# Gated cross-attention with an FFN on one core: scores of both batches in one pair, value products one tile late, variance two and FFN three tiles late inside the attention tiles, root as exp of half a log

## Chip, cores and metric

One Trainium2 chip, one core. The time is device microseconds of one execution; the kernel before has three runs and one further execution that was profiled. TensorE is called PE here, VectorE DVE, ScalarE ACT, GpSimd POOL, and SyncE SP; SP only issues DMAs.

## What is computed

`x` and `context` are 16 batches of 64 x 512 (fp32). In short:

```python
q, k = Wq @ inorm(lnorm(x)) + bq,  Wk @ inorm(ctx) + bk      # 64 x 512 per batch
v    = Ws @ ctx + bs
attn = softmax(q.T @ k)                                      # 512 x 512 per batch
mean, mean_sq = attn @ v, attn @ (v * v)
std  = sqrt(relu(mean_sq - mean * mean))
x    = x + tanh(g_xattn) * (inorm(ctx) * std + mean)
x    = x + tanh(g_ffn) * (lnorm(x) @ dequantised(weight_q).T)
```

## The kernel before

Two batches lie on the 128 partitions, so there are 8 **tiles** (t = 0 to 7). A tile's attention matrix is worked off in 8 **chunks** (c = 0 to 7) of 128 rows by 512 columns, chunks 0 to 3 of the first batch and 4 to 7 of the second. Every engine has its own program, a loop over tiles and chunks written out by hand, and semaphores tie them together; each engine takes its instructions strictly in the written order. Where a matrix is multiplied in fp32r, each operand is split into a high part `hi` and a rest `lo`, and three products (hi hi, hi lo, lo hi) replace one.

For a tile, `project` (PE) makes q and k, three products each. `keep_hi` (ACT) copies the high part out of PSUM, `keep_lo` (DVE) makes the rest. `scores` (PE) makes two chunks with six products; the two chunks run in the upper and the lower half of the array at the same time, and since both belong to the same batch, the other half needs a copy of q and k on the other partitions: `*_swapped`, made by DMAs of 128 KB that SP issues. `maximum` (DVE) takes the row maximum of a chunk, `exponentials` (ACT) the exp with its row sum, `reciprocal` (DVE) and `normalise_probs` (POOL) divide, `turn` (PE) transposes the chunk in four pieces, and `keep_turned` (ACT) copies the result from PSUM. `weigh` (PE, fp32) multiplies the turned probabilities with values and squared values. `value_product` (PE), `keep_values` (DVE) and `square_values` (POOL) make those. `keep_sums` (ACT) copies mean and mean square of one batch, each 64 x 512, into `MEAN` and `VAR`.

Then `with_mean`, `square_mean`, `variance` and `relu` run on DVE inside the next tile. The root (`root`, ACT), `scale_context` (POOL), `after_attention` and `row_statistics` (DVE), `inverse_deviation2` (POOL), `normalise_y` (ACT), `turn_y` (PE), `keep_y_hi` (ACT), `keep_y_lo` (DVE), the 12 products of `feed_forward` (PE) and `add_ffn` (DVE) all come behind the last attention tile, for all 8 tiles one after the other, because Sqrt is in another function table of ACT than Exp. The FFN weights are dequantised in tiles 6 and 7.

## Time and profile before

| | us |
|---|---|
| median of 3 runs | 201.22 (200.82 to 201.68) |
| the profiled execution, its own time | 201.95 |
| its span, first to last instruction | 200.1 |
| mean granted clock of PE | 0.991 |

The time of an execution is its span and what lies around it: 1.85 us here. The chain of waits names, for each moment of the span, what the end of the program was waiting for; the timeline gives the start and the length of each instruction of one engine, with the idle time before it and who ended that. Matmuls overlap their successors, so what one costs is read from start to start.

### The profile page before, as it was taken

The page shows a single profiled execution, that of the slowest core. Times are in us where ns is not written, and L with a number is a line of the kernel's source. Part 1 is how long each engine was busy: PE and PEld are TensorE (multiplying, and loading weights), DVE is VectorE, ACT ScalarE, POOL GpSimd, SP SyncE. Part 2 cuts the span into 40 slices and gives each one's busy share as a digit, 9 for nine tenths or more (in the row PEclk, how much of TensorE's full clock was granted, in tenths as well). Part 3 has the DMA queues.
Part 4 walks back from the last instruction along what each step waited for, and adds up shares of the span by engine and source line. Part 5 has one row for each costly group of instructions (what it writes and reads, how often), then busy time and mean ns, then how long its engine had stood idle before and what let it go on. Part 6 is the DMA issues. An engine that isn't in the chain of part 4 may idle for free.

```text
span 200.1 us, 2899 instructions
## 1 busy us (share of the span) xinstructions
PE 171.7 (86%) x816; PEld 106.3 (53%) x816; DVE 157.0 (78%) x337; ACT 127.1 (64%) x271; POOL 120.9 (60%) x143
## 2 busy tenths in 40 slices
PE   0359799999799979997997999799979893999993
PEld 0235556564465545554644565465446442787882
DVE  3868798779778976997699769955978687999751
ACT  2336767947776685959486948676594994563510
POOL 2125578458645754784487458685798957598300
PEclk9999999999999999999999999999999999699999
DMA  6247680773078127804760540073000000011322
GB/s 164 92 102 213 139 233 0 176 217 135 18 166 271 73 66 154 305 5 115 186 227 0 139 126 0 6 179 80 0 2 0 3 0 0 3 52 52 126 87 105
DMA packets 10880, 20.09 MB, mean 100 GB/s; under 512 B 1648, under 2 KB 1776, under 8 KB 10864
## 3 DMA queue, kind: packets, MB, share of 16 engines
q1 hardware_dynamic: 10864, 19.90, 35.3%
q8 instruction: 7, 0.11, 0.2%
q14 instruction: 9, 0.07, 0.1%
HBM read 9.67 MB, written 2.10 MB: 59 GB/s over the span
## 4 chain that ended last, share of the span: by engine, by line
PE 45%; DVE 26%; ACT 12%; issue 7%; DMA 3%; POOL 2%; SPq 2%; ACTq 0%; DVEq 0%
PE pv_bank L361 11%; PE score_bank L337 8%; ACT probs L484 6%; DVE neg_max L669 5%; PE turn_bank L348 5%; PE score_bank L438 4%; PE score_bank L439 4%; DVE VAR L693 4%; PE score_bank L442 4%; PE proj_bank L373 3%; DVE CTX L650 3%; DVE VAR L698 2%; ACT VAR L501 2%; DMA params_sb<-in_params 2%; DVE q_lo L663 2%
## 5 line engine op out<-in xcount | busy, mean ns | idle before, releaser
L886 POOL TENSOR_SCALAR probs<-probs,rden 128x512 f32<-128x512 f32 x64 | 56.4, 882 | 35.0 <-DVE rden L675 34.6
L484 ACT ACTIVATE probs<-score_bank,neg_max 128x512 f32<-128x512 f32 x64 | 44.3, 692 | 33.6 <-DVE neg_max L669 30.8
L361 PE MATMUL pv_bank<-probs_t,values 128*128 128x512 f32 x120 | 60.3, 604 | 0.9 <-ACT VAR L501 0.6
L669 DVE TENSOR_REDUCE neg_max<-score_bank 128x1 f32<-128x512 f32 x64 | 43.5, 681 | 20.3 <-PE score_bank L337 20.2
L348 PEld LDWEIGHTS turn_bank<-ident,probs 128*128 128x128 f32 x256 | 29.7, 142 | 26.7 <-issue 18.0
L348 PE MATMUL turn_bank<-ident,probs 128*128 128x128 f32 x256 | 37.6, 279 | 3.2 <-ACT probs_t L492 2.8
L492 ACT COPY probs_t<-turn_bank 128x512 f32<-128x512 f32 x64 | 37.3, 586 | 0.2
L361 PEld LDWEIGHTS pv_bank<-probs_t,values 128*128 128x128 f32 x120 | 19.7, 190 | 13.0 <-issue 12.5
L337 PE MATMUL score_bank<-k_hi,q_hi 64*128 64x512 f32 x32 | 16.6, 518 | 2.6 <-DVE k_lo_swapped L759 2.5
L337 PE MATMUL score_bank<-k_hi_swapped,q_hi_swapped 64*128 64x512 f32 x32 | 16.6, 518 | 0.0
L438 PE MATMUL score_bank<-w_hi,yt_hi 128*128 128x512 f32 x32 | 14.1, 440 | 0.0
L439 PE MATMUL score_bank<-w_lo,yt_hi 128*128 128x512 f32 x32 | 13.5, 423 | 0.0
L337 PE MATMUL score_bank<-k_lo_swapped,q_hi_swapped 64*128 64x512 f32 x32 | 13.0, 407 | 0.0
L337 PE MATMUL score_bank<-k_hi,q_lo 64*128 64x512 f32 x32 | 13.0, 407 | 0.0
L337 PE MATMUL score_bank<-k_lo,q_hi 64*128 64x512 f32 x32 | 13.0, 406 | 0.0
L337 PE MATMUL score_bank<-k_hi_swapped,q_lo_swapped 64*128 64x512 f32 x32 | 13.0, 406 | 0.0
L564 ACT ACTIVATE y<-X,shift,rstd 128x512 f32<-128x512 f32 x8 | 6.5, 817 | 9.9 <-POOL shift L969 9.9
L484 ACT ACTIVATION_READ_ACCUMULATOR probs<-score_bank,neg_max 128x1 f32 x64 | 12.8, 201 | 0.0
L675 DVE RECIPROCAL rden<-den 128x1 f32<-128x1 f32 x64 | 9.8, 153 | 3.5 <-ACT probs L484 2.9
L879 POOL TENSOR_TENSOR c_lo<-CTX,c_hi 128x512 fp32r<-128x512 f32 x7 | 8.9, 1271 | 5.2 <-DVE c_hi L656 5.2
L319 PE MATMUL proj_bank<-x_hi,w_qk_hi 128*128 128x512 f32 x8 | 4.6, 569 | 8.3 <-DVE x_lo L751 8.3
L337 PEld LDWEIGHTS score_bank<-k_hi,q_hi 64*128 64x128 f32 x32 | 6.2, 194 | 10.0 <-issue 6.3
(106 smaller groups left out, 343.1 us busy)
## 6 DMA issues: line engine op xcount, KB each, us to landing
X<-in_x SPq DMA_DIRECT2D x8, 256.0 KB, 3.1
CTX<-in_context SPq DMA_DIRECT2D x8, 256.0 KB, 3.4
q_hi_swapped<-q_hi SPq DMA_DIRECT2D x16, 128.0 KB, 2.3
q_lo_swapped<-q_lo SPq DMA_DIRECT2D x16, 128.0 KB, 2.4
ctx_now<-in_context SPq DMA_DIRECT2D x8, 256.0 KB, 2.6
sz<-in_scales_zeros SPq DMA_DIRECT2D x4, 512.0 KB, 4.9
out<-result SPq DMA_DIRECT2D x8, 256.0 KB, 2.0
k_hi_swapped<-k_hi SPq DMA_DIRECT2D x15, 128.0 KB, 2.4
```

Of the source, the lines that this page charges most:

```text
L337: mm = pe.matmul(score_bank[(c + half) % SBANKS][:, :], q_part[p][rows, P * j:P * j + P], k_part[p][rows, :], start=(step == 0), stop=(ste ...
L348: last = pe.transpose(turn_bank[c % 2][:, P * i:P * i + P], probs[c % SBANKS][:, P * i:P * i + P], ident[:, :])
L361: mm = pe.matmul(sums_bank(t, b)[:, :], values[:, i, b, :, :].rearrange("p a c -> p (a c)"), probs_t[b][:, i, :], start=(i == 0), stop=(i ...
L438: pe.matmul(score_bank[2 + i][:, :], hi, w_hi[:, g, :], start=(g == 0), stop=False)
L439: pe.matmul(score_bank[2 + i][:, :], hi, w_lo[:, g, :], start=False, stop=False)
L442: mm = pe.matmul(score_bank[2 + i][:, :], yt_lo[i][:, P * g:P * g + P], w_hi[:, g, :], start=False, stop=(g == GROUPS - 1))
L484: act.activation(probs[c % SBANKS][:, :], score_bank[c % SBANKS][:, :], ACT.Exp, bias=neg_max[:, c:c + 1], accum_out=den[:, c:c + 1]).then ...
L492: act.copy(probs_t[b][:, :, P * j:P * j + P], turn_bank[c % 2][:, :].rearrange("p (i n) -> p i n", i=JC)).then_inc(turned_kept, 1)
L669: dve.tensor_reduce(neg_max[:, c:c + 1], score_bank[c % SBANKS][:, :], AX_X, ALU.max, negate=True).then_inc(max_done, 1)
L675: dve.reciprocal(rden[:, c:c + 1], den[:, c:c + 1]).then_inc(rden_done, 1)
L879: pool.tensor_tensor(lo[:, :], whole, hi[:, :].bitcast(F32), ALU.subtract).then_inc(lo_done, 1)
L886: pool.tensor_scalar(probs[c % SBANKS][:, :], probs[c % SBANKS][:, :], rden[:, c:c + 1], 1.0, ALU.mult, ALU.mult).then_inc(probs_done, 1)
```

## The change

- `scores(t, p)` makes chunk pair p of **both** batches: batch 0 in the upper half of the array, batch 1 in the lower. The swapped copies, their buffers and their DMAs are gone. Chunk c now belongs to batch c % 2. A pair has a PSUM tensor of two banks (`score_banks`, two of them), and `maximum` takes both chunks in one instruction of 128 x 1024.
- `project` of q and k of tile t + 2 both stand at chunk 2 of tile t and write into `score_banks[0]`, which the scores of the pair before and after use too. So `scores(t + 1, 0)` at chunk 4 waits until `keep_lo` has read them.
- `weigh` of tile t - 1 is spread over the eight chunks of tile t. Behind the loop, `weigh` of tile 7 stands alone.
- Mean, variance and root of tile t - 2, and row statistics, stand inside tile t. Square of the mean moves from DVE to POOL; the casts `x_hi` and `c_hi` move from DVE to ACT (`split_hi`).
- The root is Exp(0.5 Ln(v)), with one function table loaded near the start by hand; v is floored at 2**-63.
- The FFN of tile t - 3 stands inside tile t: `normalise_y` at ACT's chunk 1, `turn_y` and `keep_y_hi` at chunk 2, `keep_y_lo` at chunk 3, `feed_forward` in halves at chunks 5 and 6, `add_ffn` at chunk 7. The FFN of tiles 5, 6 and 7 stands behind the loop.
- The weights are dequantised in tiles 1 and 2, the context is kept instead of loaded twice, and all loads are issued at the start.

```diff
-    AHEAD_S, AHEAD_E = 3, 2
-    SBANKS = 4
-    LAST = CHUNKS * TILES
+    AHEAD_E = 3
+    AHEAD_R = 2
+    PROBS = 6
     DMA = 16
...
+        score_banks = [banks(f"score_banks{i}", [P, 2, N]) for i in range(2)]
...
+            for t in range(1, 4):
+                load(t)
+            for g in range(GROUPS):
+                sp.dma_start(w_int[:, g, :], weight_q_t[P * g:P * g + P, :]).then_inc(ffn_w_loaded[g], DMA)
+                sp.dma_start(sz[:, g, :, :], scales_zeros[g].partition_broadcast(P)).then_inc(ffn_w_loaded[g], DMA)
+            for t in range(4, TILES):
+                load(t)
+            for u in range(TILES):
+                sp.wait_ge(result_done, u + 1)
...
+                elif t > 1:
+                    pe.wait_ge(exp_done, CHUNKS * (t - 2) + 6)
...
+            def scores(t, p):
+                number = PAIRS * t + p
+                if p == 0:
+                    pe.wait_ge(q_lo_done, t + 1)
                     pe.wait_ge(k_lo_done, t + 1)
-                if not (is_first(t) and c < SBANKS):
-                    pe.wait_ge(exp_done, CHUNKS * t + c + 2 - SBANKS)
-                for step, (q_whole, q_other, k_whole, k_other) in enumerate((
...
+                    if 2 <= t + 1 < TILES:
+                        pe.wait_ge(q_lo_done, t + 2)
+                        pe.wait_ge(k_lo_done, t + 2)
+                if number >= 2:
+                    pe.wait_ge(exp_done, 2 * (number - 2) + 2)
+                for step, (q, k) in enumerate(((q_hi, k_hi), (q_hi, k_lo), (q_lo, k_hi))):
+                    for b in range(2):
+                        rows = slice(C * b, C * b + C)
+                        mm = pe.matmul(score_banks[number % 2][:, b, :], q[t % 2][rows, P * p:P * p + P],
+                                       k[t % 2][rows, :], start=(step == 0), stop=(step == 2))
                         if step == 2:
                             mm.then_inc(scores_done, 1)
...
+                if c == 4 and t >= 3:
+                    pe.wait_ge(yt_hi_done, t - 2)
+                    pe.wait_ge(yt_lo_done, t - 2)
+                elif c == 6:
+                    pe.wait_ge(s_kept, t + 1)
+                elif CHUNKS * t + c >= 2:
+                    kept = {0: -1, 1: 0, 2: 1, 3: 3, 4: 2, 5: 5, 7: 6}[c]
+                    pe.wait_ge(turned_kept, CHUNKS * t + kept)
...
+                if (b, i) == (0, 0):
+                    pe.wait_ge(turned_kept, CHUNKS * (u + 1))
+                    pe.wait_ge(s_squared, u + 1)
...
+                    if u >= 1:
+                        pe.wait_ge(sq_kept, 2 * (u - 1) + 1)
+                    if u >= 3:
+                        pe.wait_ge(result_done, min(u - 2, TILES - 3))
...
+                pe.wait_ge(turned_kept, kept)
+                if u >= TILES - 1:
+                    pe.wait_ge(yt_hi_done, u - 1)
+                    pe.wait_ge(yt_lo_done, u - 1)
...
+                if 1 in steps:
+                    mm.then_inc(ffn_done, 1)
...
+            for t in range(TILES):
                 for c in range(CHUNKS):
-                    if c % 2 == 1 and c + AHEAD_S < CHUNKS:
-                        scores(t, c + AHEAD_S)
-                    elif c % 2 == 1 and has_next(t):
-                        scores(t + 1, c + AHEAD_S - CHUNKS)
-                    if c == 7 and has_second_next(t):
-                        pe.wait_ge(s_kept, 2 * t + 2)
+                    if c % 2 == 0:
+                        ahead = c // 2 + 2
+                        if ahead < PAIRS:
+                            scores(t, ahead)
+                        elif t + 1 < TILES:
+                            scores(t + 1, ahead - PAIRS)
+                    turn(t, c)
+                    if t > 0:
+                        weigh(t - 1, c // JC, c % JC)
+                    if c == 2 and t + 2 < TILES:
...
+                        project(t + 2, 1)
+                    if c == 2 and t >= 3:
+                        turn_y(t - 3, CHUNKS * t + 2)
+                    if c == 4:
                         value_product(t)
-            over_tiles(pe, body)
+                    if c == 5 and t >= 3:
+                        feed_forward(t - 3, 0)
+                    if c == 6 and t >= 3:
+                        feed_forward(t - 3, 1)
+            for i in range(JC):
+                weigh(TILES - 1, 0, i)
+            turn_y(TILES - 3, CHUNKS * TILES)
             for i in range(JC):
                 weigh(TILES - 1, 1, i)
...
+            feed_forward(TILES - 3, 0, 1)
+            turn_y(TILES - 2, CHUNKS * TILES)
+            feed_forward(TILES - 2, 0, 1)
+            turn_y(TILES - 1, CHUNKS * TILES)
+            feed_forward(TILES - 1, 0, 1)
...
+            def logarithm(u):
+                act.wait_ge(relu_done, u + 1)
+                act.activation(VAR[u % 2][:, :], VAR[u % 2][:, :], ACT.Ln).then_inc(log_done, 1)
...
-                act.activation(tile_of(VAR, u), tile_of(VAR, u), ACT.Sqrt).then_inc(root_done, 1)
+                act.wait_ge(log_done, u + 1)
+                act.activation(VAR[u % 2][:, :], VAR[u % 2][:, :], ACT.Exp, scale=0.5).then_inc(root_done, 1)
...
+            act.preload_act_table_set("natural_log_exp_and_others")
+            split_hi(0, 0)
+            split_hi(0, 1)
...
+            split_hi(1, 1)
+            exponentials(0, 0)
+            exponentials(0, 1)
+            keep_hi(1, 0)
+            keep_hi(1, 1)
+            exponentials(0, 2)
+            split_hi(2, 0)
+            split_hi(2, 1)
...
-                        keep_hi(t + 1, 1)
                     if c + AHEAD_E < CHUNKS:
                         exponentials(t, c + AHEAD_E)
...
+                    if c == 0 and t >= 2:
+                        keep_sums(t - 2, 1)
+                    if c == 4 and t >= 1:
                         keep_sums(t - 1, 0)
...
+                    keep_turned(t, c)
+                    if c == 1 and t >= 3:
+                        normalise_y(t - 3)
+                    if c == 2 and t >= 3:
+                        keep_y_hi(t - 3)
+                    if c == 3 and t + 2 < TILES:
                         keep_hi(t + 2, 0)
...
+                        keep_hi(t + 2, 1)
+                    if c == 5 and t >= 2:
+                        logarithm(t - 2)
+                        root(t - 2)
+                    if c == 6 and t + 3 < TILES:
+                        split_hi(t + 3, 0)
+                        split_hi(t + 3, 1)
...
+            keep_sums(TILES - 2, 1)
+            normalise_y(TILES - 3)
...
+            keep_y_hi(TILES - 3)
+            logarithm(TILES - 2)
+            root(TILES - 2)
             keep_sums(TILES - 1, 1)
-            root(5)
-            normalise_y(3)
-            root(6)
-            for u in range(2, TILES):
-                keep_y_hi(u, u % 2)
-                if u == 3:
-                    root(TILES - 1)
-                if u + 2 < TILES:
-                    normalise_y(u + 2)
+            normalise_y(TILES - 2)
+            logarithm(TILES - 1)
+            root(TILES - 1)
+            keep_y_hi(TILES - 2)
+            normalise_y(TILES - 1)
+            keep_y_hi(TILES - 1)
...
+            def maximum(t, p):
+                number = PAIRS * t + p
+                dve.wait_ge(scores_done, 2 * number + 2)
+                dve.tensor_reduce(neg_max[:, 2 * p:2 * p + 2], score_banks[number % 2][:, :, :], AX_X, ALU.max,
                                   negate=True).then_inc(max_done, 1)
...
+                    if c + AHEAD_R < CHUNKS:
+                        reciprocal(t, c + AHEAD_R)
+                    elif t + 1 < TILES:
+                        reciprocal(t + 1, c + AHEAD_R - CHUNKS)
+                    if c % 2 == 0:
+                        ahead = c // 2 + 2
+                        if ahead < PAIRS:
+                            maximum(t, ahead)
+                        elif t + 1 < TILES:
+                            maximum(t + 1, ahead - PAIRS)
+                    if c == 0 and t + 3 < TILES:
+                        statistics(t + 3, 0)
+                    if c == 1:
+                        if t + 3 < TILES:
+                            statistics(t + 3, 1)
+                        if t >= 2:
+                            with_mean(t - 2)
...
+                        if t >= 3:
+                            keep_y_lo(t - 3)
+                        if t >= 2:
+                            variance(t - 2)
+                        if t + 2 < TILES:
                             keep_lo(t + 2, 0)
...
+                            keep_lo(t + 2, 1)
+                    if c == 4 and t >= 2:
+                        relu(t - 2)
+                    if c == 5:
+                        keep_values(t)
+                        if t + 3 < TILES:
+                            normalise(t + 3, 0)
+                            normalise(t + 3, 1)
+                    if c == 7:
+                        if t >= 3:
+                            add_ffn(t - 3)
+                        if t >= 2:
+                            after_attention(t - 2)
+                            row_statistics(t - 2)
...
+            with_mean(TILES - 2)
+            variance(TILES - 2)
+            relu(TILES - 2)
+            keep_y_lo(TILES - 3)
+            after_attention(TILES - 2)
+            row_statistics(TILES - 2)
+            with_mean(TILES - 1)
+            variance(TILES - 1)
+            relu(TILES - 1)
```

On PE, the stretch around the projection of k, before. `proj_bank` holds the projection; the scores behind it are those of another pair, in another bank.

```order
L361 MATMUL pv_bank<-probs_t,values 128x512
L348 MATMUL turn_bank<-ident,probs 128x128 x8
L319 MATMUL proj_bank<-c_hi,w_qk_hi 128x512
L320 MATMUL proj_bank<-c_lo,w_qk_hi 128x512
L321 MATMUL proj_bank<-c_hi,w_qk_lo 128x512
L337 MATMUL score_bank<-k_hi_swapped,q_hi_swapped 128x512
L337 MATMUL score_bank<-k_hi,q_hi 128x512
L337 MATMUL score_bank<-k_lo_swapped,q_hi_swapped 128x512
L337 MATMUL score_bank<-k_lo,q_hi 128x512
```

The same stretch on PE in the changed kernel, in a tile with an FFN: the projection, `turn_y`, one transposed chunk, one `weigh` product and the next tile's first scores.

```order
L220 MATMUL score_banks<-c_hi,w_qk_hi 128x512
L221 MATMUL score_banks<-c_lo,w_qk_hi 128x512
L222 MATMUL score_banks<-c_hi,w_qk_lo 128x512
L293 MATMUL turn_bank<-ident,y 128x128 x4
L255 MATMUL turn_bank<-ident,probs 128x128 x4
L273 MATMUL sums_bank<-probs_t_0,values 128x512
L238 MATMUL score_banks<-k_hi,q_hi 128x512 x2
L238 MATMUL score_banks<-k_lo,q_hi 128x512 x2
L238 MATMUL score_banks<-k_hi,q_lo 128x512 x2
```

The projection's banks are now the banks of the scores four rows behind it. In between stand only eight transposes of 128 columns and one product of 512.

On ACT, before: `keep_hi` of q (L473), then exponentials, and `keep_hi` of k (L477) five rows on.

```order
L484 ACTIVATE probs,den<-score_bank,neg_max 128x512
L492 COPY probs_t<-turn_bank 128x4x128
L473 ACTIVATE q_hi<-proj_bank,params_sb 128x512
L484 ACTIVATE probs,den<-score_bank,neg_max 128x512
L500 COPY MEAN<-pv_bank 64x512
L501 COPY VAR<-pv_bank 64x512
L492 COPY probs_t<-turn_bank 128x4x128
L477 ACTIVATE k_hi<-proj_bank,params_sb 128x512
```

On ACT in the changed kernel, the same kind of stretch (chunks 2 and 3 of a tile with an FFN). L429 is `keep_y_hi`, L397 `keep_turned`, L372 `keep_hi`.

```order
L388 ACTIVATE probs,den<-score_banks,neg_max 128x512
L397 COPY probs_t_0<-turn_bank 128x4x128
L429 CAST yt_hi<-turn_bank 128x512
L388 ACTIVATE probs,den<-score_banks,neg_max 128x512
L397 COPY probs_t_1<-turn_bank 128x4x128
L372 ACTIVATE q_hi<-score_banks,params_sb 128x512
L372 ACTIVATE k_hi<-score_banks,params_sb 128x512
```

Both `keep_hi` now stand next to each other, behind a cast that waits for `turn_y`, an exponential, and a copy that waits for the transposed chunk 3.

On ACT behind the loop in the changed kernel, from the cast of the FFN of tile 5 to the end.

```order
L429 CAST yt_hi<-turn_bank 128x512
L412 ACTIVATE VAR<-VAR 128x512
L416 ACTIVATE VAR<-VAR 128x512
L407 COPY MEAN<-sums_bank 64x512
L408 COPY VAR<-sums_bank 64x512
L422 ACTIVATE y<-X,shift,rstd 128x512
L412 ACTIVATE VAR<-VAR 128x512
L416 ACTIVATE VAR<-VAR 128x512
L429 CAST yt_hi<-turn_bank 128x512
L422 ACTIVATE y<-X,shift,rstd 128x512
L429 CAST yt_hi<-turn_bank 128x512
```

L412 and L416 are log and root, first of tile 6, then of tile 7; `keep_y_hi` of tile 6 stands behind the root of tile 7.

## Rows read from the trace of the kernel before

**Rows 1.** The page, busy time of each engine over the span.
```profile
PE 171.7 (86%) x816; PEld 106.3 (53%) x816; DVE 157.0 (78%) x337; ACT 127.1 (64%) x271; POOL 120.9 (60%) x143
```

**Rows 2.** Windows: busy time of PE, PEld, DVE, ACT, POOL; clock; DMA.
```profile
71.92:90.76 18.84, 17.41 (x86) 10.21 (x86) 15.54 (x35) 13.48 (x31) 11.67 (x14) 1.00 0.50 140
165.30:200.10 34.80, 28.25 (x128) 22.37 (x128) 25.74 (x56) 13.59 (x21) 17.07 (x23) 0.95 0.16 61
```

**Rows 3.** Chain of waits in tile 5: start, length, engine, what.
```profile
109.25 0.67 DVE q_lo L663
...
110.01 0.47 PE proj_bank L319
...
110.95 0.89 PE score_bank L337 x6
...
112.43 1.72 PE pv_bank L361 x4
114.14 0.44 PE turn_bank L348 x4
...
115.44 0.89 PE proj_bank L373 x8
...
117.29 0.70 DVE neg_max L669
...
122.19 0.60 DVE mean_sq L687
...
123.47 1.59 DVE VAR L693
...
127.10 0.96 DVE VAR L698
```

**Rows 4.** Timeline of ACT in tile 3: start, length, instruction.
```profile
73.31 0.69 ACT L477 ACTIVATE k_hi<-proj_bank,params_sb 128x512 fp32r<-128x512 f32 x1 [0.28 <-PE proj_bank L321]
73.90 0.68 ACT L484 ACTIVATE probs<-score_bank,neg_max 128x512 f32<-128x512 f32 x1
...
74.56 0.58 ACT L492 COPY probs_t<-turn_bank 128x512 f32<-128x512 f32 x1
```

**Rows 5.** Timeline of PE at the start.
```profile
13.63 0.79 PE L337 MATMUL score_bank<-k_hi,q_hi 64*128 64x512 f32 x1 [2.47 <-DVE k_lo_swapped L759]
...
33.79 1.04 PE L348 MATMUL turn_bank<-ident,probs 128*128 128x128 f32 x8
```

**Rows 6.** Chain of waits behind tile 7.
```profile
158.66 1.28 ACT L506
...
159.95 0.63 ACT VAR L506
...
162.15 1.55 POOL CTX L960
...
163.73 1.75 DVE X L713
...
168.26 0.82 ACT y L564
...
180.87 0.44 PE score_bank L428 x4
...
184.10 0.44 PE score_bank L428 x4
...
196.84 0.75 DVE result L840
```

**Rows 7.** Timeline of PE behind tile 7, idle time in brackets.
```profile
167.71 0.63 PE L428 MATMUL score_bank<-ident,y 128*128 128x128 f32 x4 [2.41 <-ACT y L564]
...
169.83 0.64 PE L438 MATMUL score_bank<-w_hi,yt_hi 128*128 128x512 f32 x1
...
174.25 0.60 PE L428 MATMUL score_bank<-ident,y 128*128 128x128 f32 x4
```

**Rows 8.** The page, costliest groups: POOL's division of a chunk.
```profile
L886 POOL TENSOR_SCALAR probs<-probs,rden 128x512 f32<-128x512 f32 x64 | 56.4, 882 | 35.0 <-DVE rden L675 34.6 <-issue 0.3
```

879 lines of the change are left out of this document (318 added, 561 removed).

## The prediction, made before the changed kernel was run

> **What bounds the kernel now.** The busy times of the page come first [rows 1]: PE 86%, DVE 78%, the others about 60%. That is an average over unlike stages, so the windows come next [rows 2]. A middle tile lasts 18.84 us, DVE is busy for 15.5 of it, ACT 13.5, POOL 11.7. Behind tile 7 there are 34.8 us in which PE is busy 28.3. The chain of waits then prices PE's steps [rows 3]: a pair of scores 0.89, a turned chunk 0.44, four passes of `weigh` 1.72, which are two of its products (fp32 takes two passes), so 0.86 each, and a value product 0.89. A projection runs from 110.01 to 110.95, 0.94 where PE had idled before it, so 1.6 for two in a row. A tile has 4 x 0.89 + 8 x 0.44 + 8 x 0.86 + 0.89 + 1.6 = 16.4 us on PE. The other 2.4 us are waits, the largest for `q_lo` [rows 3], which DVE makes behind variance (1.59) and relu (0.96). So PE bounds the tiles, with one late link from ACT and DVE.
>
> **The same products, elsewhere.** The count of matmuls does not change. An FFN costs 184.10 - 180.87 = 3.23 us on PE [rows 6]. It leaves the end and makes tiles 3 to 7 longer: 16.4 + 3.2 = 19.6. The change gains only if waits become fewer. By capacity the others fit: to the windows of [rows 2] DVE adds the FFN's rest and sum, residual and statistics (about 3.5, at 0.6 to 0.75 each as in [rows 3, 6]) and loses two casts and a square (about 2), which makes 17; ACT adds two casts, log, root, y and its cast, some 3.8, which makes 17.3; POOL adds a square, a scaling (1.55, [rows 6]) and two powers, some 3.5, which makes 15. All stay under 19.6. What decides is the order.
>
> **The link at chunk 4.** `project` writes into the banks that `scores(t + 1, 0)` needs. Count from P, the end of both projections. In tiles 1 and 2 PE has a turn and a `weigh` to do, 0.44 + 0.86 = 1.3 us. Meanwhile ACT cannot start `keep_hi` before it has copied chunk 3, turned at P + 0.6, so the copy (0.58) ends at P + 1.15; `keep_hi` twice at a pitch of 73.90 - 73.31 = 0.59, the second ends at P + 2.4 [rows 4]; `keep_lo` of k 0.67 and a semaphore: P + 3.2. PE waits 1.9. In tiles 3 to 5 `turn_y` stands in front (P + 0.6), ACT casts it (0.5), then takes exponential 6 (0.66), the copy of chunk 3 (0.5), `keep_hi` twice (1.3), DVE takes `keep_lo` (0.7), and semaphores add 0.15: P + 4.4. PE has 1.74 us of work, so it waits 2.7. Exponential 6 could run earlier only if it stood ahead of the cast, which it does not. This wait takes the place of the one for `q_lo` and is as long.
>
> Elsewhere in a tile the chain just fits: residual and statistics of tile t - 3 end 1.3 us into the next tile, the two-chunk maximum (2 x 0.60, a little less than 0.70 twice) ends at 2.6, exponentials 4 and 5 with `normalise_y` between them at 5.4, and the projection wants them at 5.7. I add 0.3 per tile for this. The double maximum saves some 0.1 a pair on DVE, which is not waited for: nothing. The DMAs that go (swapped copies) held only tile 0 back.
>
> **Start.** Before, the first scores run at 13.63, after two swapping copies of 0.8 in series [rows 5]. These go, but the second table load stands before the cast of x: 1.28 us by row [rows 6]. The two cancel; first scores again at 13.6. The Trainium skill ("ScalarE: Activation LUTs", What ACT_TABLE_LOAD costs) puts a switch of tables at 2.66 us with its drain; here the next activation starts 0.01 us behind the 1.28. By the page the start would be 1.4 us later. Then tile 0, counted down each queue: maximum of the first pair 16.3, of the second, behind a set of statistics, 18.4, first division on POOL 20.3 (behind a second set), DVE's `keep_lo` and `normalise` of tiles 1 and 2 until 22.3, POOL's two rests of tile 2 (1.27 each, an estimate next to its 1.55) until 24.9, turned chunk 2 at 26.1, projections of tile 2 at 27.8, next scores at 30.9, and 4.5 us for the rest of tile 0: tile 1 starts at **35.4**. Before, that point is 33.79 + 0.44 = 34.2 [rows 5].
>
> **Sum.** Tile 1: 16.4 + 1.9 at chunk 4 + 1.4 because `weigh` of tile 0 waits for its last copied chunk = 19.7. Tile 2: 16.4 + 1.9 + 0.5 (POOL has weights, rests and square there, some 18 to 19 us) = 18.8. Tiles 3 to 5: 19.6 + 2.7 + 0.3 = 22.6 each, 67.8. Tile 6 without projection: 16.4 - 1.6 + 3.2 + 0.2 = 18.2. Tile 7, two pairs of scores fewer: 16.4. The loop ends at 35.4 + 19.7 + 18.8 + 67.8 + 18.2 + 16.4 = **176.3**.
>
> Behind it `weigh` of tile 7 and one `turn_y` take 7.3, and ACT copies the sums until 8.7. But tile 7 queues behind tile 6: cast for tile 5 at 5.3, log and root of tile 6 (2 x 0.63) 6.6, scaling, residual, statistics, power 10.7, then POOL squares tile 7's mean 11.8, variance and relu 13.0, log and root 14.3. From scaling to y the chain of before took 162.15 to 169.08, 6.9 us, with the residual at 1.75 and another tile's statistics in it [rows 6]; freed of these I count 4.9: y at 19.2. Turn 0.6, cast 0.6, twelve products 2.9, sum 0.75: 24.2. The store and end are 200.1 - 197.6 = 2.5. PE idles about 2.8 us ahead of the FFN of tile 6. Before, it idled 2.41, turned a tile, and ran at half rate from 169.83 to 174.25, 4.4 us for what takes 2.8 at full rate [rows 7]; the granted clock of the stretch is 0.95, that of a tile 1.00 [rows 2], so PE fell from 2.4 to 1.2 GHz for that time. I take 1.2 us, since the last FFN may be back at full rate. The tail is 27.9, the span 176.3 + 27.9 = **204.2**. The profiled execution of before was 201.95 with a span of 200.1, and the median 0.73 under it: 204.2 + 1.85 - 0.73 = **205.3 us**, 2% slower. The bounds: the tail's 4.9 may be 6.9 (+2) or the clock may stay up (-1.2); the waits of six tiles are together 15 us, and half a microsecond each way is 3; tile 0 is known to about 2. Added as squares that is about 4: 201 to 209.5 for this case alone.
>
> **Rivals.**
> *Faster.* The wait at chunk 4 is short. It holds if ACT and DVE run ahead enough that `keep_lo` of k ends by P + 2; then tiles are 19.7 with FFN, six waits of 1.9 to 2.7 become 0.3, which takes 12 us off: 193. For it speaks the spare capacity; against it, that copy and both `keep_hi` must follow P in any case, 3 us of rows. Half of it is possible, 199. It decides from 0.7 us less in each of six tiles on: that is the 4 us to the time of before. Chance 0.2.
> *No change.* Waits at chunk 4 of 2 instead of 2.7, tail without the half rate: 201 to 202. Chance 0.15.
> *DVE and POOL slow each other.* Two products of one shape take 0.60 and 1.59 in before, and POOL's division 0.88 in the mean [rows 3, 8]. With more on both, residual and with_mean at 1.75 would lie on the way to exponential 5: 1 us more in each of five tiles and in the tail: 211. That two-input DVE work and POOL share their way to SBUF is also what the Trainium skill says ("GPSIMD Engine Reference", Key points). Against it: most of what stands there reads PSUM. Chance 0.15.
> *The clock falls inside tiles.* The wait of 2.7 is longer than the 2.41 of [rows 7]. If PE falls to half rate behind it, a tile loses about 2: 210. Chance 0.1.
> *The root does not do what it says*, tables reloaded around each log: two loads of 1.28 a tile on ACT. The instructions in order hold only two loads in all. Below 0.01.
> The forecast keeps 0.4.
>
> **How the numbers follow.** A difference under 0.5% can't be told from none with this kernel. Faster by more: 0.2, from the first rival. Same: 0.15. Slower: 0.65. The range is 197 to 211: it leaves out the deeper half of the first rival and the worst of the slow ones.
>
> **What would show it.** In the trace after: PE waits of 1.9 (tiles 1, 2) and 2.7 us (3 to 5) in front of the first scores of a tile, ended by `keep_lo` of k; tile starts about 22.6 apart in tiles 3 to 5; tile 1 starting at 35; 28 us behind tile 7's last turned chunk, with ACT's root and POOL's scaling on the chain. Wrong if tiles are near 20 apart, or if the wait at chunk 4 is ended by something else.

## The result

The changed kernel takes **226.35 us** (median of 4 runs, 226.26 to 226.62); beside it the kernel before took 201.30 (200.82 to 201.68). The ratio is 1.125, 95% interval 1.122 to 1.127. The forecast was 205.3 us with a range of 197 to 211: the direction was right, the loss six times as large as forecast (25.0 us against 4.1). The profiled execution took 226.42 us, with a span of 224.4. Medians here and below are of all runs of a kernel; ratios and their intervals leave out single executions that were over 1.5% above the kernel's fastest.

The page of the kernel after, to be held against [rows 1]:

```profile
span 224.4 us, 2734 instructions
## 1 busy us (share of the span) xinstructions
PE 179.9 (80%) x816; PEld 112.2 (50%) x816; DVE 135.2 (60%) x275; ACT 138.5 (62%) x292; POOL 119.2 (53%) x149
...
PEclk9999576999998899979996799969999999999589
```

No engine is busy for a larger share than before; DVE's share fell from 78% to 60%. So this is not a kernel with too much work on one engine. The last line is the one to look at: the granted clock drops again and again between the start and the tail (a 5, 6, 7 or 8 among the 9s).

Tiles, as windows from the first `scores(t, 2)` of a tile to that of the next (tiles 2 to 6, last row: behind the loop). Columns as in [rows 2]: window, length, busy time of PE, PEld, DVE, ACT, POOL, granted clock, DMA share, GB/s.

```profile
59.45:80.56 21.11, 18.52 (x88) 10.69 (x88) 16.78 (x30) 15.31 (x35) 17.93 (x19) 0.92 0.00 1
80.56:107.72 27.16, 22.21 (x103) 13.37 (x102) 18.71 (x35) 17.68 (x40) 19.19 (x22) 0.94 0.00 1
107.72:133.56 25.84, 23.07 (x103) 14.65 (x102) 15.81 (x34) 16.77 (x37) 13.64 (x17) 0.87 0.03 11
133.56:158.09 24.53, 21.76 (x103) 13.70 (x102) 12.32 (x26) 15.84 (x35) 10.99 (x14) 0.93 0.03 11
158.09:176.77 18.68, 18.68 (x98) 11.43 (x97) 10.92 (x24) 14.68 (x33) 9.78 (x13) 1.00 0.04 14
...
193.80:224.40 30.60, 19.80 (x66) 12.09 (x64) 13.40 (x28) 10.45 (x17) 7.62 (x10) 0.89 0.09 35
```

Forecast were 18.8 us for tile 2, 22.6 for tiles 3 to 5, 18.2 for tile 6, 27.9 for the tail. Tile 6 fits. Tiles 2 to 5 are 2.3, 4.6, 3.2 and 1.9 us longer, and those are the tiles with a clock under 1.00. Tile 4 shows why. PE's timeline there (start, length, instruction, in brackets its idle time and who ended it):

```profile
115.01 0.60 PE L293 MATMUL turn_bank<-ident,y 128*128 128x128 f32 x4
115.44 0.60 PE L255 MATMUL turn_bank<-ident,probs 128*128 128x128 f32 x4
115.88 1.02 PE L273 MATMUL sums_bank<-probs_t,values 128*128 128x512 f32 x2
119.67 0.79 PE L238 MATMUL score_banks<-k_hi,q_hi 64*128 64x512 f32 x2 [2.77 <-DVE k_lo L518]
120.24 0.66 PE L238 MATMUL score_banks<-k_lo,q_hi 64*128 64x512 f32 x2
120.66 0.66 PE L238 MATMUL score_banks<-k_hi,q_lo 64*128 64x512 f32 x2
121.25 1.12 PE L255 MATMUL turn_bank<-ident,probs 128*128 128x128 f32 x4
122.16 1.92 PE L273 MATMUL sums_bank<-probs_t,values 128*128 128x512 f32 x2
123.87 1.92 PE L282 MATMUL turn_bank<-params_sb,CTX 128*128 128x128 f32 x8
```

Two things stand in these rows. The projections end at P = 115.01 and the next scores start at P + 4.66, behind a wait of 2.77 us that `k_lo` ends; forecast were P + 4.4 and 2.7. Behind the wait every product takes about twice as long: turning a chunk goes from 0.60 to 1.12, `weigh` from 1.02 to 1.92. PE had idled, and came back at 1.2 GHz instead of 2.4: from 119.7 to 125.6 us the granted clock is 0.50. The chain of waits gives the steps of the link:

```profile
116.91 0.48 ACT probs_t L397
117.39 0.60 ACT q_hi L372
...
118.01 0.75 DVE q_lo L518
118.76 0.67 DVE k_lo L518
...
119.67 1.62 PE score_banks L238 x5
```

It is the chain that the prediction counted. All six such waits: 2.91, 2.04, 2.59, 2.77, 2.77, 2.77 us (tiles 0 to 5), 15.85 in sum, all ended by `k_lo`. The low clock follows those of tiles 0, 2, 3, 4 and 5, and not that of tile 1, the shortest.

### The profile page after: what moved, and what is told of

Its sections match the earlier page's. It is cut to its first block, busy times and chain, and to the rows that moved or that the text cites. A ratio compares the mean times of both kernels' runs of the same rounds, so it can differ in the third digit from the quotient of the medians.

```text
span 224.4 us, 2734 instructions
## 1 busy us (share of the span) xinstructions
PE 179.9 (80%) x816; PEld 112.2 (50%) x816; DVE 135.2 (60%) x275; ACT 138.5 (62%) x292; POOL 119.2 (53%) x149
## 3 DMA queue, kind: packets, MB, share of 16 engines
q1 hardware_dynamic: 4752, 9.67, 11.8%
## 4 chain that ended last, share of the span: by engine, by line
PE 55%; DVE 17%; issue 9%; ACT 7%; POOL 7%; DMA 2%; SPq 0%; ACTq 0%; POOLq 0%; DVEq 0%
PE sums_bank L273 15%; PE turn_bank L255 11%; PE score_banks L238 11%; PE turn_bank L282 4%; DVE k_lo L518 2%; DVE neg_max L524 2%; DVE q_lo L518 2%; DMA params_sb<-in_params 2%; POOL CTXN L733 2%; ACT q_hi L372 2%; PE sums_bank L320 2%; PE sums_bank L314 2%; ACT probs L388 1%; PE score_banks L314 1%; DVE CTXN L511 1%
## 5 line engine op out<-in xcount | busy, mean ns | idle before, releaser
L273 PE MATMUL sums_bank<-probs_t,values 128*128 128x512 f32 x128 | 67.7, 620 | 1.0 <-ACT probs_t L397 1.0
L397 ACT COPY probs_t<-turn_bank 128x512 f32<-128x512 f32 x64 | 37.4, 585 | 39.5 <-PE turn_bank L255 39.3
L524 DVE TENSOR_REDUCE neg_max<-score_banks 128x2 f32<-128x1024 f32 x32 | 38.8, 1212 | 19.8 <-PE score_banks L238 19.8
L388 ACT ACTIVATE probs<-score_banks,neg_max 128x512 f32<-128x512 f32 x64 | 44.3, 693 | 7.5 <-DVE neg_max L524 7.2
L255 PEld LDWEIGHTS turn_bank<-ident,probs 128*128 128x128 f32 x256 | 31.6, 151 | 24.4 <-issue 12.6
L238 PE MATMUL score_banks<-k_hi,q_hi 64*128 64x512 f32 x64 | 17.4, 534 | 18.5 <-DVE k_lo L518 17.5
L238 PEld LDWEIGHTS score_banks<-k_hi,q_hi 64*128 64x128 f32 x64 | 6.7, 200 | 38.1 <-DVE q_lo L518 20.2
L273 PEld LDWEIGHTS sums_bank<-probs_t,values 128*128 128x128 f32 x128 | 20.8, 200 | 4.7 <-issue 2.9
L238 PE MATMUL score_banks<-k_hi,q_lo 64*128 64x512 f32 x64 | 14.4, 435 | 0.0
L733 POOL TENSOR_TENSOR CTXN<-CTXN,VAR 128x512 f32<-128x512 f32 x8 | 10.2, 1273 | 7.7 <-ACT VAR L416 7.7
L238 PE MATMUL score_banks<-k_lo,q_hi 64*128 64x512 f32 x64 | 14.2, 431 | 0.0
L282 PEld LDWEIGHTS turn_bank<-params_sb,CTX 128*128 128x128 f32 x64 | 10.9, 241 | 5.3 <-issue 5.3
L536 DVE TENSOR_TENSOR values<-turn_bank,params_sb 128x512 f32<-128x512 f32 x8 | 5.5, 691 | 13.2 <-PE turn_bank L282 13.2
L388 ACT ACTIVATION_READ_ACCUMULATOR probs<-score_banks,neg_max 128x1 f32 x64 | 13.1, 205 | 0.0
L282 PE MATMUL turn_bank<-params_sb,CTX 128*128 128x128 f32 x64 | 10.6, 320 | 0.0
```

The costliest lines, as they stand in the source:

```text
L238: mm = pe.matmul(score_banks[number % 2][:, b, :], q[t % 2][rows, P * p:P * p + P], k[t % 2][rows, :], start=(step == 0), stop=(step == 2))
L255: last = pe.transpose(bank[:, P * i:P * i + P], probs[(CHUNKS * t + c) % PROBS][:, P * i:P * i + P], ident[:, :])
L273: mm = pe.matmul(sums_bank[b][:, :], values[u % 2][:, i, b, :, :].rearrange("p a c -> p (a c)"), probs_t[u % 2][b][:, i, :], start=(i == 0 ...
L282: last = pe.matmul(turn_bank[0][:, P * i:P * i + P], CTX[:, t, P * i:P * i + P], w_s, start=True, stop=True)
L388: act.activation(probs[g % PROBS][:, :], score_banks[(g // 2) % 2][:, g % 2, :], ACT.Exp, bias=neg_max[:, c:c + 1], accum_out=den[:, c:c + ...
L397: act.copy(probs_t[t % 2][b][:, :, P * j:P * j + P], bank[:, :].rearrange("p (i n) -> p i n", i=JC)).then_inc(turned_kept, 1)
```

## The experiments

**Theory.** The wait in front of a tile's first scores costs twice: its own length, and the half rate behind it. **Rivals:** DVE and POOL slow each other, and the clock only mirrors the idle time; the FFN inside the tiles is simply too much work. Each kernel below is the changed kernel with small edits, from "The weights, elsewhere" on always on top of both halves of the link moved; "P" is again the end of both projections of a tile. The kernel before ran beside them (medians of 201.3 to 201.6).

### Fill the wait, keep the order

Added on PE (work for nothing; the results are those of the kernel):

```diff
+            def fill(t, n):
+                pe.wait_ge(k_lo_done, 2)
+                if t >= 2:
+                    pe.wait_ge(sq_kept, 2 * (t - 1))
+                for _ in range(n):
+                    pe.matmul(sums_bank[1][:, :], w_qk_hi[:, 0, :], q_hi[(t + 1) % 2][:, :], start=True, stop=True)
...
+                    if c == 3 and t + 2 < TILES:
+                        fill(t, (13, 8, 8, 12, 12, 12)[t])
```

> The kernel after, with 8 to 13 products of 512 columns added on PE at the end of chunk 3 of tiles 0 to 5, into a bank that is free then; nothing reads them, so they are work for nothing. They fill most of the wait in front of the next tile's first scores and leave the order of everything else. Main theory (the wait costs twice: its own 2.0 to 2.9 us, and the clock that falls behind it): the scores start as late as before, counted from the projections, but run at full rate; granted clock 1.00 in tiles 2 to 5 instead of 0.87 to 0.94; tile 4 falls from 25.8 to about 23, and the whole from 226.3 to about 214 (some 2.9 us in each of tiles 0, 3, 4 and 5, 1.6 in tile 2). Rival 1 (what is slow is DVE and POOL in each other's way; the clock only mirrors idle time): tiles stay as long, 226. Rival 2 (the added products hold something up, since sums_bank[1] or the queue was not free): above 226.

Measured: **216.19 us** (215.05 to 218.65), ratio 1.071 [1.065, 1.077]. PE in tile 4:

```profile
108.90 0.60 PE L300 MATMUL turn_bank<-ident,y 128*128 128x128 f32 x4
...
110.23 3.37 PE L291 MATMUL sums_bank<-q_hi,w_qk_hi 128*128 128x512 f32 x12
113.57 0.50 PE L238 MATMUL score_banks<-k_hi,q_hi 64*128 64x512 f32 x2
113.88 0.42 PE L238 MATMUL score_banks<-k_lo,q_hi 64*128 64x512 f32 x2
114.11 0.42 PE L238 MATMUL score_banks<-k_hi,q_lo 64*128 64x512 f32 x2
114.46 0.66 PE L255 MATMUL turn_bank<-ident,probs 128*128 128x128 f32 x4
```

The scores start at P + 4.67, where they started before, so the link is as late as it was. But they run 0.23 us apart instead of 0.42, and the tile takes 22.9 us instead of 25.8. From those scores to the `weigh` of chunk 5 it is 3.57 us against 6.51: the half rate cost 2.9 us in this tile. PE did more work, the link came no earlier, and 10 us went away over the kernel. The rival by which the clock only mirrors idle time is out. The Trainium skill ("TensorE: Matmul & The Clock Gate", Wait — 56ns, not 53.3ns?) gives 426.7 and 215.7 ns from start to start of products of 512 columns at the two clocks; the pitch of 0.42 us agrees, that of 0.23 is 7% above the page's.

The same reading for all six tiles, from a tile's first scores (those of tile t + 1) to the end of its window: 6.33, 8.17, 9.78, 12.50, 13.89 and 12.58 us in the kernel after, 4.80, 8.18, 8.16, 10.95, 10.95 and 10.96 with the fill. The half rate costs 1.5 to 1.6 us in tiles 0, 2, 3 and 5, 2.9 in tile 4 and nothing in tile 1: **9.3 us** together. The profiled execution with the fill also reached `scores(0, 2)` 0.85 us earlier (17.22 against 18.07), where nothing was changed; starts differ that much from one execution to the next.

### Fill it in doses

The same edit with `(0, 0, 0, 3, 6, 9)` products.

> The kernel after, with 3, 6 and 9 products added (work for nothing, as in e1_fill) at the end of chunk 3 of tiles 3, 4 and 5, none in tiles 0 to 2: the wait of 2.77 us in front of the next scores is cut to about 2.1, 1.5 and 0.8. Theory (half rate follows the wait, and only a long one): behind 0.8 and 1.5 the scores run at full rate, tiles 4 and 5 at 22.9 instead of 25.8 and 24.5; behind 2.1 it may go either way, since behind 2.04 it stayed and behind 2.09 it fell in earlier runs. Whole 226.35 - 1.6 - 2.9 = about 222, or 220 if tile 3 is freed too. Rival (any idle time at that place makes PE fall): tiles as in after, 226.

Measured: 222.93 us median; its four runs lie far apart (218.08 to 226.03), so the time alone decides little. The profiled one took 220.44. The first scores behind tiles 3, 4 and 5 in it:

```profile
94.83 0.50 PE L238 MATMUL score_banks<-k_hi,q_hi 64*128 64x512 f32 x2 [2.08 <-DVE k_lo L527]
...
117.73 0.51 PE L238 MATMUL score_banks<-k_hi,q_hi 64*128 64x512 f32 x2 [1.37 <-DVE k_lo L527]
...
140.64 0.50 PE L238 MATMUL score_banks<-k_hi,q_hi 64*128 64x512 f32 x2 [0.67 <-DVE k_lo L527]
```

Behind 2.08, 1.37 and 0.67 all is at full rate, and tiles 4 and 5 take 22.90 each. In this execution three products (0.7 us) in tile 3 were enough to keep the clock, while tile 2 of the same run, with its wait of 2.60, fell to half rate as ever. The rival that any idle time there makes PE fall is out. That these doses always suffice is not shown: two of the four executions took 225.43 and 226.03 us with a mean granted clock of 0.93, as the kernel after has, and of those there is no trace.

### Move ACT's half of the link

```diff
-                    if c == 2 and t >= 3:
-                        keep_y_hi(t - 3)
-                    if c == 3 and t + 2 < TILES:
+                    if c == 2 and t + 2 < TILES:
                         keep_hi(t + 2, 0)
                         keep_hi(t + 2, 1)
+                    if c == 2 and t >= 3:
+                        keep_y_hi(t - 3)
```

> The kernel after, with only ACT's two casts keep_hi moved from chunk 3 to chunk 2, ahead of keep_y_hi; DVE keeps its order (keep_y_lo, variance, keep_lo twice in chunk 3). Main theory: in tiles 0 to 2, with no y to cast, the casts end at P + 1.2 instead of P + 2.4, the scores wait 0.7 to 1 us instead of 2.0 to 2.9, and the clock does not fall: 1.3 less in each and 3 and 1.6 us of half rate less in tiles 0 and 2. In tiles 3 to 5 the cast of y now stands behind both, and DVE's rest of y and variance stand ahead of keep_lo, so the wait stays near 2.7 and half rate stays behind it. Whole about 218. Rival (ACT alone makes the link): all six waits shrink to under 1, whole about 205. Rival (the clock falls for another reason than this wait): half rate stays in tiles 0 and 2, about 222.

Measured: **218.8 us** (217.12 to 219.5), ratio 1.084 [1.078, 1.091]. The waits are now 1.33, 0.47, 2.09, 2.81, 2.37, 2.37. In tiles 0 and 1 the link is short, as expected. In tile 2 it is 2.09, more than the 0.7 to 1 I had written: there `variance` (1.10 us) already stands ahead of `keep_lo` on DVE. In tiles 3 to 5 DVE's order holds the link, as its chain behind tile 4 shows:

```profile
109.64 0.58 ACT yt_hi L429
...
110.86 0.68 DVE VAR L549
111.54 0.66 DVE q_lo L518
112.20 0.67 DVE k_lo L518
...
113.11 1.19 PE score_banks L238 x3
```

Both casts end early, and `keep_lo` still waits for the rest of y and for variance. The rival by which ACT alone makes the link is out. Half rate stays behind 2.81, 2.37, 2.37, and here behind 2.09 too (the turned chunk at 66.02 us takes 1.11).

### Move both halves

The edit above, and on DVE:

```diff
+                    if c == 2 and t + 2 < TILES:
+                        keep_lo(t + 2, 0)
+                        keep_lo(t + 2, 1)
                     if c == 3:
...
-                        if t + 2 < TILES:
-                            keep_lo(t + 2, 0)
-                            keep_lo(t + 2, 1)
```

> The kernel after, with keep_hi on ACT and keep_lo on DVE both moved to chunk 2, ahead of the cast and the rest of y and of variance. Same work, another order. Main theory: k_lo ends at P + 2.0, PE has 1.3 to 1.9 us of work until then, so the wait is under 0.5, PE stays at full rate, and both costs go: tiles 3, 4, 5 at about 21.5, 20.2, 20 us, tile 1 starts at 33 to 34, whole about 199 (15.8 us of waits and some 12 of half rate less). Rival 1 (the half rate is not a consequence of the wait): only the waits go, about 210. Rival 2 (capacity or contention of DVE and POOL is the bound behind the link): the waits come back elsewhere in the tile, 218 or more.

Measured: **204.97 us** (204.52 to 206.86), ratio 1.019 [1.012, 1.025]. PE behind tile 4's projections, to be held against the rows of the kernel after:

```profile
103.31 0.60 PE L293 MATMUL turn_bank<-ident,y 128*128 128x128 f32 x4
103.75 0.60 PE L255 MATMUL turn_bank<-ident,probs 128*128 128x128 f32 x4
104.18 1.02 PE L273 MATMUL sums_bank<-probs_t,values 128*128 128x512 f32 x2
105.24 0.50 PE L238 MATMUL score_banks<-k_hi,q_hi 64*128 64x512 f32 x2
```

No wait: the scores start at P + 1.93. On DVE the two rests go ahead of that of y:

```profile
103.55 0.75 DVE L518 SCALAR_TENSOR_TENSOR q_lo<-score_banks,params_sb,q_hi 128x512 fp32r<-128x512 f32 x1 [0.82 <-ACT q_hi L372]
104.23 0.75 DVE L518 SCALAR_TENSOR_TENSOR k_lo<-score_banks,params_sb,k_hi 128x512 fp32r<-128x512 f32 x1
...
104.97 0.67 DVE L586 TENSOR_TENSOR yt_lo<-turn_bank,yt_hi 128x512 fp32r<-128x512 f32 x1
```

Four instructions a tile in another place give back 21.4 of the 25 us, with the same work. Tiles 3 and 4 as windows:

```profile
71.65:96.03 24.38, 20.93 (x103) 12.46 (x103) 19.59 (x37) 18.52 (x41) 20.18 (x23) 1.00 0.00 1
96.03:116.19 20.16, 20.13 (x103) 12.61 (x103) 15.77 (x34) 16.89 (x37) 13.66 (x17) 1.00 0.04 14
```

Tile 4 is now PE's own work, 20.13 busy of 20.16, near the 19.9 that the prediction counts without the wait. It is 6 us more than the 199 expected: tile 3 takes 24.4 instead of 21.5, and tile 1 starts at 35.5 instead of 33 to 34. Tile 3 is the one place where capacity shows: POOL is busy for 20.2 of it and DVE for 19.6, and PE waits there for POOL:

```profile
79.31 0.66 PE L255 MATMUL turn_bank<-ident,probs 128*128 128x128 f32 x4 [1.12 <-POOL probs L706]
...
81.69 0.47 PE L220 MATMUL score_banks<-x_hi,w_qk_hi 128*128 128x512 f32 x1 [0.87 <-ACT probs L388]
```

The same two waits, 1.12 and 0.87, stand in the kernel after (at 86.70 and 89.09). Two more stand in front of them here, 0.59 and 0.83 for chunks 0 and 1; in the kernel after, chunk 1 waits for 0.19. In all PE waits 3.4 us in this tile.

### The weights, elsewhere

The weights in tiles 0 and 1 instead of 1 and 2 (DVE's part; POOL's `dequantise` and `weights_lo` likewise):

```diff
-                    if t in (1, 2):
+                    if t in (0, 1):
                         if c in (1, 5):
-                            scale_weights(2 * (t - 1) + c // 4)
+                            scale_weights(2 * t + c // 4)
```

> The order of the kernel before this one (casts and rests at chunk 2), and the weights of the FFN dequantised in tiles 0 and 1 instead of 1 and 2. Theory: the waits for POOL's probabilities at the start of tile 3 (1.12 and 0.19 us, 0.87 for an exponential) come from the last weights at the end of tile 2 and go, but part returns in tile 1: 1 to 2 us under the kernel with the link alone, about 197.5. Rival: those waits come from tile 3's own work, and nothing changes (within 0.5 us), or tile 0, where POOL is late already, gets longer by as much as tile 3 gains.

Measured: **202.76 us** (201.95 to 204.15), ratio 1.007 [1.003, 1.010]. Tile 3 falls from 24.38 to 20.36, tile 1 grows from 18.62 to 20.91: both sentences of the expectation hold in part, and 2.2 us stay. Not all of tile 1's growth is the weights' work. The kernel of "Behind the last tile" has the same tile 1, and the two traces show the `weigh` of its first chunk behind the same wait, the first line here, the second there:

```profile
38.17 2.04 PE L273 MATMUL sums_bank<-probs_t,values 128*128 128x512 f32 x2 [0.96 <-ACT probs_t L397]
37.27 1.12 PE L273 MATMUL sums_bank<-probs_t,values 128*128 128x512 f32 x2 [0.96 <-ACT probs_t L397]
```

Here PE ran on at half rate until about 42 us (granted clock 0.57 from 38 to 42), there it did not (1.00), and that tile 1 takes 19.68. So the weights cost tile 1 about 1.1 us, and half rate another 1.2, in some executions only. Then the four groups placed in the first halves of tiles 0 and 2 and both halves of tile 1:

```diff
+    GROUP_AT = [(0, 0), (1, 0), (1, 1), (2, 0)]
...
-                    if t in (0, 1):
+                    if (t, c // 4) in GROUP_AT:
                         if c in (1, 5):
-                            scale_weights(2 * t + c // 4)
+                            scale_weights(GROUP_AT.index((t, c // 4)))
```

> The kernel e4_link_weights with only the four groups of weights placed elsewhere: the first halves of tiles 0 and 2, both halves of tile 1 (there they were the halves of tiles 0 and 1). In the runs so far tile 3 took 24.4 us with a group in the second half of tile 2 and 20.4 without, tile 1 took 20.9 with one in the second half of tile 0 and 18.6 without; tile 2, behind a group in the second half of tile 1, took the same either way. Theory (a group that POOL and DVE work on across a tile's boundary holds up the next tile's probabilities, and tiles 0 and 2 have no room for it): tiles 1, 2, 3 at 18.6, 17.5, 20.4, whole 202.8 - 2.2 = about 200.5. Rival (each group costs the same wherever it is): 202.8.

Measured: 202.96 us (201.31 to 204.69), ratio 1.003 [1.000, 1.007]: nothing over the placement before. Tiles 1 and 2 take 18.63 and 17.51 as expected, but tile 3 is 21.89 and not 20.4, with a wait of 1.20 for an exponential. My rule, that only a group across a tile's boundary costs, is wrong in that form. The 2.3 us by which tile 1 is shorter hold the 1.2 of half rate, so the work itself gained 1.1 there and lost 1.5 in tile 3.

### Behind the last tile

POOL and DVE there, with the weights as in the first of the two placements:

```diff
-            with_mean(TILES - 1)
             variance(TILES - 1)
             relu(TILES - 1)
+            with_mean(TILES - 1)
...
-            inverse_deviation2(TILES - 2)
             square_mean(TILES - 1)
+            inverse_deviation2(TILES - 2)
```

> The kernel e4_link_weights with another order behind the last tile only: POOL squares tile 7's mean ahead of the power for tile 6 (it waited for that power from 178.9 to 181.7), and DVE takes variance and relu of tile 7 ahead of adding its mean. Theory (the tail is a chain through POOL's and DVE's queues, not PE's work): mean_sq ends at 180.0 instead of 182.8, the cast of y for tile 6 follows 1.5 us earlier, and y of tile 7 comes 2.5 to 3 us earlier; PE idles 2 instead of 3.5 us ahead of the FFN of tile 6. Whole 202.8 - 3 = about 199.8. Rival (PE bounds the tail: FFN at half rate): the last FFN starts no earlier than the one before it ends, gain under 1 us, 202.

Measured: **200.29 us** (199.1 to 202.7), ratio 0.990 [0.984, 0.995]. POOL in the kernel without this edit:

```profile
180.52 0.99 POOL L739 TENSOR_TENSOR rstd<-var_eps,power 128x1 f32<-128x1 f32 x1 [2.06 <-DVE var_eps L571]
...
181.72 1.04 POOL L728 TENSOR_TENSOR mean_sq<-MEAN 128x512 f32<-128x512 f32 x1
```

and with it:

```profile
176.78 1.21 POOL L728 TENSOR_TENSOR mean_sq<-MEAN 128x512 f32<-128x512 f32 x1 [0.48 <-ACT MEAN L407]
178.36 1.01 POOL L739 TENSOR_TENSOR rstd<-var_eps,power 128x1 f32<-128x1 f32 x1 [0.37 <-DVE var_eps L571]
```

Counted from the last turned chunk (168.83 and 166.68), `mean_sq` of tile 7 starts 10.1 instead of 12.9 us behind it, and the tail is 30.4 instead of 32.2 us. These 1.8 us are the edit's; the rest of the difference between the two traces lies ahead of it, 0.9 in the start and tile 0, 1.2 in tile 1's half rate. PE idles 1.95 instead of 3.50 us ahead of the FFN of tile 6, and that FFN is still at half rate for most of its length. Both edits together:

> Both edits of e5_tail and e6_spread. If they act in different places they add: 202.8 - 3.0 - 2.2 = about 197.6, under the 201.3 of the kernel before all changes; if the new order of work (FFN in the tiles, root by exp and log) costs more than it gives once its waits are gone, it stays at or over 201.

Measured: 201.40 us (200.66 to 202.95), ratio 0.999 [0.995, 1.002]. The tail's order takes 1.6 us off this placement too (202.96 to 201.40). But the expected 197.6 is missed: the new placement of the weights brings nothing here either.

### Dummy work at the start and in the tail

```diff
+            pe.wait_ge(ident_ready, 1)
+            for _ in range(40):
+                pe.matmul(turn_bank[1][:, 0:P], ident[:, :], ident[:, :], start=True, stop=True)
             pe.wait_ge(w_split, 1)
             project(0, 0)
```

> The kernel e7_both with 40 products of the identity with itself (128 columns, nothing reads them) on PE ahead of the first projection, while it has nothing else to do (from about 1.5 us to 8.4 us). In the runs so far PE starts at half rate at 8.4 us and stays there until 17.7. Theory (PE comes up to 2.4 GHz by having worked, whatever the work): projections and first scores run at full rate, the first scores start about 1 us earlier, tile 0 by 2; whole about 2 us under e7_both, 195.6. Rival (the low rate at the start belongs to the first microseconds, not to idleness): the start keeps its half rate and the products delay it, 0 to 2 us over e7_both.

Measured: 202.76 us (201.39 to 204.72), ratio 1.002 [0.999, 1.006]. The 40 products ran from 1.55 to 13.2 us and held the first projection up, which then took 0.40 instead of 0.63 us a product. So the rate was full behind them, as the theory had it, and the delay ate up what that gave. With 22 of them, ahead of the kernel with the new tail:

> The kernel e5_tail with 22 products of the identity with itself (nothing reads them) on PE ahead of the first projection. In e8_head_fill 40 of them ran from 1.55 to 13.2 us at full clock, about 0.29 us each, so they held the first projection up by 5 us, but what followed them ran at full rate and the whole was only 1.4 us longer. Now 22 should end at 8 us, when the first operand is ready. Theory: projections and first scores at full rate, first scores 1.2 us earlier, tile 0's second half free of the half rate; whole 1.5 to 2.5 us under e5_tail's 200.3, about 198.3. Rival (head waits for DVE and POOL, not for PE): within 0.5 us of e5_tail.

Measured: 199.77 us (198.55 to 201.62), ratio 0.992 [0.989, 0.995], no different from 0.990 without them. The rival holds. The start of PE in this kernel:

```profile
12.26 0.50 PE L238 MATMUL score_banks<-k_hi,q_hi 64*128 64x512 f32 x2 [1.81 <-DVE k_lo L521]
...
13.28 0.61 PE L238 MATMUL score_banks<-k_lo,q_hi 64*128 64x512 f32 x2
...
14.63 0.79 PE L220 MATMUL sums_bank<-x_hi,w_qk_hi 128*128 128x512 f32 x1 [0.32 <-POOL x_lo L704]
```

The first scores come at 12.3, behind a wait for DVE, and PE falls back to half rate at 13.3 us, 1 us behind a wait of 1.81; the products of the next tile's operands then wait for POOL. The nine traces whose kernels have no such products have their first scores between 12.5 and 13.9, so 12.3 tells little. Last, 6 products in front of `turn_y` of tile 6 and 6 behind it:

```diff
+            pe.wait_ge(sq_kept, 2 * TILES)
+            for _ in range(6):
+                pe.matmul(sums_bank[0][:, 0:P], ident[:, :], ident[:, :], start=True, stop=True)
             turn_y(TILES - 2, CHUNKS * TILES)
+            for _ in range(6):
+                pe.matmul(sums_bank[0][:, 0:P], ident[:, :], ident[:, :], start=True, stop=True)
             feed_forward(TILES - 2, 0, 1)
```

> The kernel e9_head_22 with 6 more such products in front of turn_y of tile 6 and 6 behind it, in PE's idle 2.10 and 1.95 us. Theory: the FFN of tile 6 runs at full rate (1.0 us less), ends before y of tile 7 is ready, and the turn of y for tile 7 comes 0.8 us earlier: whole 0.8 us under e9_head_22. Rival (y of tile 7 sets the end anyway, or the products delay the turn): no gain or a loss under 0.5 us.

Measured: 199.70 us (197.93 to 201.36), ratio 0.989 [0.984, 0.994]. Beside 199.77 that isn't told apart from nothing. In its profile the FFN of tile 6 is at full rate and the last FFN starts 1.0 us earlier (189.74 instead of 190.78). Half of this lies ahead of the tail. The other half is PE's: without the products `turn_y` of tile 7 starts at 188.68, right behind the half-rate FFN, 0.6 us after y is ready (188.07); with them it follows y at once (187.53, 187.59). From there on the chain through y of tile 7 sets the end. The start of this execution, whose head is that of the kernel with 22 products, is a second look at it: PE stayed at full rate up to its third pair of scores, and that pair came at 17.30, against 17.17 in the other. So the start does wait for DVE and POOL, not for PE's rate.

## Why the prediction was wrong, step by step

- **The failed step** is the sum's term for tiles 2 to 5, "2.7 + 0.3" (1.9 in tile 2): the wait was counted by its length only. That PE comes back from it at half rate stood among the rivals, "The clock falls inside tiles", with a chance of 0.1 and 2 us a tile. It belonged in the forecast: [rows 7] show PE at half rate behind 2.41 us of idle time, and the forecast itself put 2.7 into each of three tiles. I used that row for the tail and not for the loop. Half rate behind these waits costs 9.3 us, 1.5 in tile 0 and the rest in tiles 2 to 5, and filling the waits takes 10.2 off the whole (226.35 - 216.19). With the waits as long as ever but filled, tiles 4 and 5 take 22.90 each, against the 22.6 of the forecast.
- **A reading beside it** was wrong too. The prediction says that the new wait is as long as the one for `q_lo` before. Before, that wait is 1.36 to 1.38 us in every tile from 2 to 6, half as long, and PE runs at full rate behind it (0.40 us a product, the clock of a tile 1.00 [rows 2]):

```profile
110.01 0.47 PE L319 MATMUL proj_bank<-c_hi,w_qk_hi 128*128 128x512 f32 x1 [1.37 <-DVE q_lo L663]
```

- **Where the 20.2 us are** between the forecast span of 204.2 and the measured 224.4: 9.3 are half rate behind the six waits, 2.4 more lie in the start and tile 0, 2.7 in tile 3 ahead of its projections (10.0 us from the tile's start to their end, against 7.3 in tiles 2, 4 and 5), 2.7 in the tail. The remaining 3 are parts of 0.3 to 0.7 in single tiles.
- **The link at chunk 4** was right: P + 4.66 against 4.4, waits of 2.77 against 2.7, for tile 1 2.04 against 1.9. Tile 2 had 2.59 instead of 1.9, since variance stands in front there too.
- **What the link costs in all**: with both halves moved, 21.4 us. The waits in front of first scores go from 15.85 to 2.37 us (1.32, 0.46, 0.59), which is 13.5, and the 9.3 of half rate go with them; tile 3 takes 1.5 more ahead of its projections. The waits' own length is the larger price, half rate adds two thirds of it.
- **The first rival** ("the wait at chunk 4 is short", 193) priced the opposite of this: it takes six waits away and gives 12 us. That kernel, once made, runs at 205.0. Its saving beside the kernel after is larger than priced, and its end is higher, because tile 3 and the tail are longer than I had them.
- **DVE and POOL in each other's way** (211): not on the whole. POOL's division takes 0.734 in the mean against 0.882 before [rows 8], variance 0.74 against the 1.59 of [rows 3]. In tile 3 single divisions do take 1.13 instead of 0.69, and PE waits there for POOL and an exponential, 2.2 us in the kernel after; how much of that is the one slowing the other and how much the amount of work (POOL is busy for 19 us) no run separates. Moving the weights took 4.0 off tile 3 and gave 1.1 of it back in tile 1, 2.3 where the clock fell too. The prediction had given that work 0.5, to tile 2.
- **Capacity**: right but for tile 3. Once the waits are gone, tiles 4 and 5 take 20.2 us, 19.9 by the forecast's terms; tiles 6 and 7 took 18.7 and 17.0 against 18.2 and 16.4.
- **The start**: the 1.28 of the table load was right, the cast of x starts at once behind it. First scores came at 13.47 against 13.6; as they come between 12.5 and 13.9 with this head, part of that is luck. Tile 1 starts at 39.3 instead of 35.4. The projections of tile 2 end at 29.0 instead of 27.8, the next scores follow 3.97 us later instead of 3.1, behind a wait of 2.91, and the rest of the tile takes 6.3 instead of 4.5, of which 1.5 is half rate. Of these 3.9 us the link gave back 3.8 (35.5).
- **The tail**: 30.6 against 27.9. y of tile 7 is ready 20.7 us behind the loop instead of 19.2: the cast for tile 5 ends at 6.2 instead of 5.3 and POOL's power for tile 6, with the shift behind it, at 12.1 instead of 10.7, so its square for tile 7, which stands behind that power, ends at 13.1 instead of 11.8. The sum from y on left out `keep_y_lo` (0.69), and the store took 3.0 instead of 2.5. The half rate of the tail was right: `turn_y` of tile 7 starts 1.0 us after its y, behind the slow FFN, against the 1.2 of the forecast. Squaring tile 7's mean ahead of that power gives 1.8 us in the traces; the medians go from 202.76 to 200.29.

So the change as made loses 25 us, most of it to four instructions' places in two queues. With those moved, the weights one tile earlier and POOL's order in the tail, the same design is at 200.3, 1% under the kernel before (ratio 0.990, interval 0.984 to 0.995). That is the fastest order tried here that adds no dummy work. PE is still idle for 9.9 of the tail's 30.4 us; what part of that can be had was not tried.

## What to carry to other kernels

A wait on PE can have two prices, and the second is paid behind it: when a sum puts a wait of some 2.5 us into every tile, look in the trace for what PE did behind its longest idle time, and put that into each tile of the sum, not among the rivals. To tell the two prices apart, fill the wait with dummy products and leave the order alone: what then goes away is the clock's part. And where one bank of PSUM serves both a projection and the next scores, try the instructions that empty it first in every queue, ahead of whatever else has become ready; here that gave 21.4 of 226 us.
